# Three of thirteen groups take their destination rows by a gather instead of by one-hot matmuls

## What is computed

```python
row, col = (edge_index[0], edge_index[1])
ef = jnp.concatenate([x[row], x[col], edge_attr], axis=-1)
h = ef @ W1 + b1
mu = jnp.mean(h, axis=0)
var = jnp.mean((h - mu) ** 2, axis=0)
h = (h - mu) * jax.lax.rsqrt(var + BN_EPS) * gamma + beta
h = jax.nn.relu(h)
msgs = h @ W2 + b2
sums = jax.ops.segment_sum(msgs, row, num_segments=n_nodes)
```

## Time and profile before

| | |
|---|---|
| median of 3 runs | 3950.47 us (3949.36 to 3950.79) |
| the profiled execution | 3951.36 us, its span 3949.5 us |
| TensorE busy | 3769.3 us, 95% |
| VectorE busy | 2573.1 us, 65% |
| ScalarE busy | 1395.4 us, 35% |
| GpSimd busy | 85.1 us, 2% |
| chain that ended last | TensorE 91%, VectorE 4% |
| 128-column matmuls of p and q in the pass (L1296, L1298) | 7056 each on the four banks |

### The profile page before, as it was taken

How to read it: one execution, slowest core, us unless ns; L and a number is a source line. 1 busy time by engine, 2 the same in 40 slices (tenths; PEclk the granted TensorE clock), 3 DMA queues, 4 the chain that set the end, 5 groups by cost and what they waited for, 6 DMA issues and landing times.

```text
span 3949.5 us, 104146 instructions
## 1 busy us (share of the span) xinstructions
PE 3769.3 (95%) x42510; PEld 2695.9 (68%) x42510; DVE 2573.1 (65%) x3609; ACT 1395.4 (35%) x3527; POOL 85.1 (2%) x53
## 2 busy tenths in 40 slices
PE   4699999999998799999999999997999999999999
PEld 3488888888887688887888888884444444454444
DVE  7999999999993688888888888875111111111222
ACT  5355555545543355554555455545000000000000
POOL 0000000000000000000000000000000000000000
PEclk9899999999998899999999999999999999999999
DMA  7123223232233733333333333334666566656664
GB/s 238 51 83 99 84 87 93 84 96 88 81 98 140 122 126 129 133 122 125 124 132 131 124 126 129 126 114 144 196 196 197 188 199 196 196 189 207 211 204 139
DMA packets 397700, 547.34 MB, mean 139 GB/s; under 512 B 175743, under 2 KB 335240, under 8 KB 390440
## 3 DMA queue, kind: packets, MB, share of 16 engines
q1 hardware_dynamic: 390856, 537.51, 42.9%
q10 hardware_dynamic: 6624, 6.42, 0.5%
HBM read 434.34 MB, written 109.53 MB: 138 GB/s over the span
## 4 chain that ended last, share of the span: by engine, by line
PE 91%; DVE 4%; SPq 2%; ACT 1%; issue 1%; DMA 1%; ACTq 0%; DVEq 0%
PE py L1579 29%; PE pY L835 10%; PE ph L1298 10%; PE ph L1296 10%; PE pSum L1312 10%; PE pbk L896 8%; PE pA L822 3%; PE ph L1291 3%; PE pX L827 2%; PE pS L826 1%; PE pbk L873 1%; PE ptr L881 1%; DVE prod_raw L1120 1%; PE pg L1567 1%; SPq L1245 1%
## 5 line engine op out<-in xcount | busy, mean ns | idle before, releaser
L1579 PE MATMUL py<-ring_raw,p 128*128 128x512 bf16 (+1 forms) x3822 | 783.4, 367 | 18.0 <-DVE dummy L1739 16.1
L1298 PE MATMUL ph<-q,prod_raw 128*128 128x128 bf16 x7056 | 781.7, 220 | 0.8 <-issue 0.8
L1296 PE MATMUL ph<-p,prod_raw 128*128 (+1 forms) x7056 | 780.9, 220 | 0.0
L1579 PEld LDWEIGHTS py<-ring_raw,p 128*128 128x128 bf16 x3822 | 362.2, 98 | 430.9 <-DVE dummy L1739 16.5
L1296 PEld LDWEIGHTS ph<-p,prod_raw 128*128 128x128 bf16 x7056 | 518.6, 98 | 110.9 <-issue 2.7
L1347 ACT ACTIVATE x<-ph 128x512 bf16<-128x512 f32 x588 | 351.2, 597 | 668.0 <-PE ph L1298 664.7
L1439 DVE SCALAR_TENSOR_TENSOR ring_raw<-ph,x 128x512 f32<-128x512 f32 x588 | 404.3, 688 | 182.0 <-ACT x L1347 170.8
L1312 PE MATMUL pSum<-x,ring_raw 128*128 128x384 bf16 x2401 | 499.6, 327 | 8.9 <-DVE x L1444 8.9
L835 PE MATMUL pY<-p,ring_raw 128*128 128x128 bf16 x7203 | 501.0, 219 | 0.2 <-issue 0.2
L1298 PEld LDWEIGHTS ph<-q,prod_raw 128*128 128x128 bf16 x7056 | 495.8, 98 | 0.0
L1755 DVE TENSOR_TENSOR yt<-py,dinv_row 128x512 f32<-128x512 f32 (+1 forms) x39 | 25.8, 661 | 697.1 <-PE py L1579 697.1
(11 more groups left out here) (322 smaller groups left out, 3906.0 us busy)
## 6 DMA issues: line engine op xcount, KB each, us to landing
ring_raw<-at_dram SPq DMA_DIRECT2D x252, 896.0 KB, 4.8
prod_raw<-lrow_dram SPq DMA_DIRECT2D x147, 768.0 KB, 4.2
at_dram<-ring_raw SPq DMA_DIRECT2D x49, 1568.0 KB, 5.6
prod_raw<-lrow_dram SPq DMA_DIRECT2D x49, 832.0 KB, 4.3
arow_dram<-x SPq DMA_DIRECT2D x147, 73.5 KB
x<-arow_dram SPq DMA_DIRECT2D x147, 54.0 KB
q<-q_dram SPq DMA_DIRECT2D x1, 4704.0 KB, 25.6
ring_raw<-at_dram SPq DMA_DIRECT2D x21, 224.0 KB, 2.5
```

The lines of the kernel that those rows point to most:

```text
L1296: nc.tensor.matmul(bank[:, k * P:(k + 1) * P], T[q][:, 0, at:at + P], p_b[:, :, m3, :].rearrange("p a d -> p (a d)"), start=False, stop=False)
L1298: last = nc.tensor.matmul(bank[:, k * P:(k + 1) * P], T[q][:, 1, at:at + P], q3[:, c, m3, :], start=False, stop=m3 == 2 and k == w - 1)
L1579: last = nc.tensor.matmul(py[par][:, 0:w], g3[c % 2][:, 7 * i + m, k, :], ring[i][:, 0:w // P, m, :], start=i == m == k == 0, stop=i == m ...
```

## The change

TAKEN = (2, 5, 8): one group in each of the first three quarters. In these TensorE issues no q matmuls. GpSimd gathers the float32 q rows of the group's four cells from pq_dram, one row of 512 bytes per slot, four gathers of 128 rows per group, and VectorE adds them to the bank's content (add_q); the sum goes to res, and relu and left read res instead of the bank.

- The T buffers of the first three quarters need the destinations of 8 cells instead of 12: the compare has 2560 columns instead of 3072, and the load is two transfers instead of one.
- The places of the three groups in q3 are not loaded; they hold the gathered rows (q_rows, 8 D of 12 D bfloat16 columns) and the table of row numbers (taken_rows).
- The row numbers come from pass one: ScalarE copies the local destination numbers too (tgt_all), between lo_all and cells, and after its last diagonal GpSimd adds the base of the block in three operations. The load of q3 is four transfers, for 37 of 49 cells.
- In pass two GpSimd copies four numbers per partition as integers (chosen) and issues four gathers, for group i of block b as soon as the add of group i in block b - 1 is done.
- The order on ScalarE and VectorE at a taken group is another one: ScalarE issues middle(g - 1) first, waits for the add, and then does the relu; VectorE issues the add, low(g - 1), left(g).

```diff
+TAKEN = (2, 5, 8)
+THOTS = tuple(sum(4 if g < 12 else 1 for g in range(lo, hi) if g not in TAKEN) for lo, hi in QUARTERS)
...
+            hole = [q3_flat[:, 12 * D * g:12 * D * (g + 1)] for g in TAKEN]
+            q_rows = [h[:, 0:8 * D].bitcast(F32).rearrange("p (c d) -> p c d", d=D) for h in hole]
...
-                            sp.dma_start(q3[:], q3_dram).then_inc(S["q3_in"], 16)
+                            for lo, hi in zip([0] + [4 * g + 4 for g in TAKEN], [4 * g for g in TAKEN] + [B]):
+                                sp.dma_start(q3[:, lo:hi, :, :], q3_dram[:, lo:hi, :, :]).then_inc(S["q3_in"], 16)
...
+                    for i, g in enumerate(TAKEN):
+                        base = row_base[:, 4 * g:4 * g + 4].unsqueeze(1).to_broadcast([P, B, 4])
+                        nc.gpsimd.tensor_tensor(taken_rows[i], tgt_all[:, 4 * g:4 * g + 4, :].rearrange("p c b -> p b c"), base, ALU.add).then_inc(S["a_final"], 1)
...
+                            nc.scalar.activation(tgt_all[:, s:s + 1, :] if isinstance(s, int) else tgt_all[:, bass.ds(s, 1), :], got[:, 1:2, :], ACT.Copy)
...
+                    def gather(b, i):
+                        row = taken_rows[i][:, b:b + 1, :] if isinstance(b, int) else taken_rows[i][:, bass.ds(b, 1), :]
+                        nc.gpsimd.tensor_copy(chosen[i][:].unsqueeze(1), row).then_inc(S["rows_chosen"], 1)
+                        put(pool, S["rows_chosen"], b * len(TAKEN) + (i + 1))
+                        for k in range(4):
+                            nc.gpsimd.indirect_dma_start(q_rows[i][:, k, :], None, pq_rows, bass.IndirectOffsetOnAxis(ap=chosen[i][:, k:k + 1], axis=0)).then_inc(q_rows_in[i], 16)
...
-                            for m3 in range(3):
+                            for m3 in range(0 if g in TAKEN else 3):
                                 last = nc.tensor.matmul(bank[:, k * P:(k + 1) * P], T[q][:, 1, at:at + P], q3[:, c, m3, :], start=False, stop=m3 == 2 and k == w - 1)
...
+                            if g in TAKEN:
+                                middle(b, g - 1)
+                                act.wait_ge(S["q_added"], b * len(TAKEN) + (TAKEN.index(g) + 1))
+                                hidden = res[which(g)][:, 0:w, :]
...
-                        dve.wait_ge(t_in[k], b * 16 + 16)
-                        V.tensor_scalar(T[k], T[k], pid1[:, 0:1], None, ALU.is_equal).then_inc(S["t_ready"], 1)
+                        dve.wait_ge(t_in[k], b * T_IN[k] + T_IN[k])
+                        places = T[k].rearrange("p f s -> p (f s)")[:, 0:(QCELLS[k] + THOTS[k]) * P]
+                        V.tensor_scalar(places, places, pid1[:, 0:1], None, ALU.is_equal).then_inc(S["t_ready"], 1)
...
+                    def add_q(b, g):
+                        u, i = which(g), TAKEN.index(g)
+                        dve.wait_ge(S["mm_done"], b * 13 + (g + 1))
+                        dve.wait_ge(q_rows_in[i], b * 64 + 64)
+                        V.tensor_tensor(res[u], banks[u].rearrange("p (c d) -> p c d", d=D), q_rows[i], ALU.add).then_inc(S["q_added"], 1)
...
+                            if g in TAKEN:
+                                add_q(b, g)
+                                low(b, g - 1)
                             left(b, g)
```

More of the change, by code:

```diff
@@ L613, in build @@
             q3_flat = q3[:].rearrange("p b m d -> p (b m d)")
+            hole = [q3_flat[:, 12 * D * g:12 * D * (g + 1)] for g in TAKEN]
+            q_rows = [h[:, 0:8 * D].bitcast(F32).rearrange("p (c d) -> p c d", d=D) for h in hole]
+            taken_rows = [h[:, 8 * D:8 * D + 8 * B].bitcast(F32).rearrange("p (b c) -> p b c", c=4) for h in hole]
             prod_raw = sb("prod_raw", [P, 2 * 4 * TPB * B], BF16)
@@ L1203, in build @@
                 st = ps("st", [P, 512])
+                chosen = [sb(f"chosen{i}", [P, 4], I32) for i in range(len(TAKEN))]
+                pq_rows = pq_dram.rearrange("a r d -> (a r) d")
+                T_IN = tuple(16 + 16 * (QCELLS[k] != THOTS[k]) for k in range(4))
                 def which(g):
@@ L1256, in pool_2 @@
                     pool.wait_ge(S["rows_set"], 1)
+                    def gather(b, i):
[4 more added lines that the diff above has]
+                            nc.gpsimd.indirect_dma_start(q_rows[i][:, k, :], None, pq_rows, bass.IndirectOffsetOnAxis(ap=chosen[i][:, k:k + 1], axis=0)).then_inc(q_rows_in[i], 16)
+                    for i in range(len(TAKEN)):
+                        gather(0, i)
+                    with pool.Fori(1, B) as b:
+                        for i in range(len(TAKEN)):
+                            put(pool, S["q_added"], b * len(TAKEN) + (i + 1 - len(TAKEN)))
+                            gather(b, i)
                 def pe_2(pe):
@@ L1295, in hidden @@
                             for m3 in range(3):
-                                nc.tensor.matmul(bank[:, k * P:(k + 1) * P], T[q][:, 0, at:at + P], p_b[:, :, m3, :].rearrange("p a d -> p (a d)"), start=False, stop=False)
-                            for m3 in range(3):
+                                last = nc.tensor.matmul(bank[:, k * P:(k + 1) * P], T[q][:, 0, at:at + P], p_b[:, :, m3, :].rearrange("p a d -> p (a d)"), start=False, stop=g in TAKEN and m3 == 2 and k == w - 1)
+                            for m3 in range(0 if g in TAKEN else 3):
                                 last = nc.tensor.matmul(bank[:, k * P:(k + 1) * P], T[q][:, 1, at:at + P], q3[:, c, m3, :], start=False, stop=m3 == 2 and k == w - 1)
@@ L1344, in one_block @@
                             w = len(group(g))
-                            act.wait_ge(S["mm_done"], b * 13 + (g + 1))
+                            if g in TAKEN:
+                                middle(b, g - 1)
+                                act.wait_ge(S["q_added"], b * len(TAKEN) + (TAKEN.index(g) + 1))
+                                hidden = res[which(g)][:, 0:w, :]
+                            else:
+                                act.wait_ge(S["mm_done"], b * 13 + (g + 1))
+                                hidden = banks[which(g)][:, 0:w * P].rearrange("p (c d) -> p c d", d=D)
                             bank_free(act, S["sum_done"], b, g)
-                            nc.scalar.activation(zb[which(g)][:, 0:w, 0, :], banks[which(g)][:, 0:w * P].rearrange("p (c d) -> p c d", d=D), ACT.Relu).then_inc(S["z_hi"], 1)
-                            if g >= 1:
+                            nc.scalar.activation(zb[which(g)][:, 0:w, 0, :], hidden, ACT.Relu).then_inc(S["z_hi"], 1)
+                            if g in TAKEN:
+                                pass
+                            elif g >= 1:
                                 middle(b, g - 1)
```

32 lines of the change are left out of this document (24 added, 8 removed).

## The result

The changed kernel took **4026.9 us** (median of 4 runs, 4021.2 to 4027.7) against 3950.5 us: 1.9% slower, ratio 1.0186 with a 95% interval of 1.0174 to 1.0199. The forecast was 3967 us. Its sign came out as forecast and the time lies in its range, but the loss was 76 us instead of 16.

What follows compares the result with a forecast made beforehand. TensorE was taken to pace pass two at 27.11 us a block, VectorE afterwards at 27.38; 3951.4 + 13.0 (blocks) + 7.2 (pass-one copy) - 3.8 (load) = 3967.8, forecast 3967 us, 0.4% slower, range 3915 to 4060.

Steps and rivals of the forecast that it cites:

- TensorE's saving: In pass two, three groups lose 12 q matmuls each: 2.01 us a block, leaving 25.10 us for TensorE alone.
- VectorE's loop: In pass two, VectorE's chain from left(1) to the next left(1) becomes the pace: 26.66 us a block, before the copies.
- The three copies: GpSimd's row-number copies in pass two delay VectorE by 0.24 us each, 0.72 a block, making it 27.38.
- the copies cost nothing: Rival, 20%: GpSimd's row-number copies in pass two do not delay VectorE; the block stays 26.66 us, total 3932 us.
- That rival's second figure: With free row-number copies in pass two and half of VectorE's 1.11 us of round-trip holes gone: 3915 us.
- Gathers priced at nothing: In pass two, GpSimd's twelve gathers a block take 0 from VectorE, with 0.42 us each as upper bound.
- The sign: Whole kernel: the change was forecast slower, by 0.4%, with 55% for slower by more than 0.2%.
- gathers hold the compares: Rival, 20%: in pass two, gathers in progress delay VectorE's three compares a block by 0.42 us each, 60 more: 4027 us.
- its own sign: In pass two, blocks of 28 us and more with compares longer than 0.9 us would show gathers holding them.
- GpSimd as the pace: Rival, 13%: in pass two, gathers longer than 1.9 us make GpSimd the pace; at 2.2 us, 31.3 a block, 4155 us.
- Pass one: ScalarE's extra copy adds 0.15 us a step, +7.2 us; the shorter q3 load at its end saves 3.8 us.

## Where the prediction was right and where wrong

- **TensorE's saving: right.** 25.10 us was priced for TensorE alone, 25.09 and 25.07 were measured in the two kernels that leave VectorE's adds out.
- **VectorE's loop: right as a mechanism, short by 0.2 to 0.3.** It was priced at 26.66 us without the copies and measured at 26.91 to 26.93 in four kernels with on-time signals, the single block mostly at 26.85. One turn of it, in the change with empty instructions (left of group 1, add, low, left of group 2; then low of group 9, the sums of group 9, the next left of group 1):

```profile
2024.47 0.69 DVE L1495 SCALAR_TENSOR_TENSOR ring_raw<-ph,x 128x512 f32<-128x512 f32 x1 [0.94 <-ACT x L1393]
...
2025.68 0.69 DVE L1489 TENSOR_TENSOR ring_raw<-ph,q 128x512 f32<-128x512 f32 x1
2026.28 0.68 DVE L1500 TENSOR_TENSOR x<-ring_raw,x 128x512 bf16<-128x512 f32 x1
2027.14 0.69 DVE L1495 SCALAR_TENSOR_TENSOR ring_raw<-ring_raw,x 128x512 f32<-128x512 f32 x1 [0.18 <-ACT x L1393]
...
2045.24 0.68 DVE L1500 TENSOR_TENSOR x<-ring_raw,x 128x512 bf16<-128x512 f32 x1
...
2051.32 0.69 DVE L1495 SCALAR_TENSOR_TENSOR ring_raw<-ph,x 128x512 f32<-128x512 f32 x1 [0.94 <-ACT x L1393]
```

```profile
2045.98 0.83 PE L1352 MATMUL pSum<-x,ring_raw 128*128 128x384 bf16 x4 [0.59 <-DVE x L1500]
```

  From left to the sums of group 9 it is 21.51 us, where 20.16 + 1.11 + 0.13 = 21.40 was counted; from there to the next left 5.34 for 4.42 + 0.84 = 5.26. The turn is 26.85. The hole before the second left is 0.26 (2027.14 - 2026.28 - 0.60) for the 0.17 of the count. The 0.08 from there to the mean of 26.93 come from two longer blocks (35.0 and 34.3 us, the 16th and the 32nd) less a short last one (15.0); each kernel has them, the one before too (33.4, 31.7, 16.4), and nothing here explains them.
- **The three copies: wrong, they cost VectorE nothing.** 0.24 each was taken from the one-hot beside GpSimd's add. In the turn above low starts 0.60 after the add with the copy behind it, and 0.60 or 0.61 after it in every block from 1400 to 2600 us, there and in the changed kernel. The copy is the one that gets longer: 0.41 us beside VectorE, 0.19 at the least. The rival "the copies cost nothing" had the right mechanism, and its 3932 us is 7 us off the 3939.4 that the change takes without late signals. The row that I took the price from had two large operations; here four numbers a partition stand against them. That rival's second figure, 3915 with half of the holes gone, is wrong by its own terms: half of 1.11 us over 48 blocks is 27 us, which gives 3905.
- **Gathers priced at nothing: this step failed, in a way no rival had.** "For a gather I take 0 on VectorE" is true of VectorE. What the sum left out is that another engine's signals can be held up: it had no term for a wait that lasts longer than the work it waits for. The late signals cost 48 x (28.51 - 26.93) = 76 us in the blocks and 8 in the statistics, 84 together; the change with the empty instructions is 88 us faster than the one without.
- **The sign was luck.** "Slower" rested on the copies' 0.72 us a block, which VectorE doesn't lose. Without the late signals, which the sum did not have, the change is 0.27% faster than before, and the forecast of 0.4% slower would have had the wrong sign.
- **The rival "gathers hold the compares"** gave 4027 us, the time that was measured, and is refuted all the same: the compare took 0.88 us beside gathers, plain transfers and nothing alike, and the loss stayed with no add in the loop. In the changed kernel 47 of the 147 short compares start while a gather is under way, and they take 0.877 to 0.883 us with no idle time before them. A number that fits proves no mechanism; its own sign, compares above 0.9 us, stood in the prediction and did not appear. The Trainium skill (SBUF — State Buffer, Who interferes with whom) would have VectorE's tensor_scalar in a two-port mode and GpSimd's descriptor writing exclude each other; no run here shows that on VectorE. On GpSimd, in the change with empty instructions, gathers beside a compare take 1.02 us in the median and the others 0.95; why they do is not shown. The same section of the Trainium skill says of TensorE and ScalarE that they never wait on anyone. Of SBUF's ports this case shows nothing to the contrary; but TensorE's signals came late here.
- **GpSimd as the pace: rightly at the edge.** Gathers take 0.94 to 1.68 us, and GpSimd is busy 52% of the stretch above.
- **Pass one.** The forecast was +7.2 for the copy and -3.8 for the load. The first and last starts of that step's copy:

```profile
L1012 ACT ACTIVATE x<-pbk x49: 392/395/400, 120.5 to 1207.0; 128x49 f32 x42, 128x49 bf16<-128x49 f32 x7
```

  1086.5 us for 48 steps against 1083.9 (120.7 to 1204.6) before: 0.05 a step, not 0.15, +2.6 us. At its end TensorE's wait behind the row loads went from 11.6 to 9.2 us, -2.4. Together 0 where +3.4 was counted.

The sum as it came out: -97 (TensorE) + 88 (adds and their loop, 1.84 x 48) + 76 (late signals in the blocks) + 8 or 9 (late signals in the statistics) = +76.

What stays open: why an instruction between two indirect transfers lets TensorE's signals through. In the changed kernel, where the rows of two groups can follow each other closely, 39 late signals with relu right behind them are due during a first gather and others between gathers, so "second to fourth" is the pattern of one group alone. Why the same loop takes 28.5 or 27.8 us a block was not followed. Whether other engines' signals would be late in another kernel, or only TensorE's, was not tried; nor were indirect transfers of another size.

## What to carry to other kernels

When an engine that was idle gets work, price not only what it takes from its neighbours' operations but what it may do to their signals: compare the start of each waiting operation with the end of what releases it, and read a "remote" releaser on a wait that has one known source as a signal that came late. If GpSimd makes several indirect transfers one behind the other, put an empty instruction or a wait between them, and look at the release times again. And find out with one kernel that leaves the suspect out whether a cost is there, before believing a sum that happens to fit: both 4027 (compares held) and 27.58 (costs per group) fitted to the digit and were wrong.

## What the runs showed of the hardware

- With four indirect transfers of 128 rows of 512 bytes one behind the other on GpSimd, TensorE's mm_done signals came up to 2.1 us late with one such row a block and up to 3.3 with three; with plain transfers of the same bytes, with one empty instruction between, or with a wait between, they came 14 to 16 ns after the matmul's modelled end. With two in a row they came up to 1.5 us late. In the kernels with rows the trace also lacks records of other engines' signals, in the changed kernel 140 of relu's 540 and 76 of the compare's 166.
- Such a transfer holds GpSimd for 0.94 us at the least and up to 1.68 us in the changed kernel (2.50 in the one with gathers and no adds), a plain one of the same size for 0.54. The Trainium skill (DMA: Bandwidth & Descriptors, Latency and other measured facts) puts a GpSimd transfer's first byte at about 1 us; the traces have the 0.94 us for the indirect instruction on GpSimd, and no run here shows when the first byte comes.
- An empty instruction on GpSimd between two indirect transfers cost no time: the gap stayed 0.30 us.
- A float32 add of 128x512 with one operand in PSUM takes 0.68 us with the next operation 0.60 behind it, as subtractions of that shape do.
- Two kernels with the same loop, in which only the instant of the first gathers differs, ran at 28.51 and 27.77 us a block.
